# Opening, last unit and tail of a fused attention and recurrent layer: rotation halves interleaved, key stack split, two batches' output products moved

## Time and profile before

| | |
|---|---|
| median of three runs | 5033.72 us (5031.82 to 5034.27) |
| profiled execution | 5053.02 us, span 5051.2 us |
| mean granted PE clock | 0.986 |
| PE busy | 4895.6 us (97%) |
| DVE busy | 3960.6 us (78%) |
| ACT busy | 2884.9 us (57%) |
| POOL busy | 2930.4 us (58%) |

### The profile page before, as it was taken

How to read it: one execution, slowest core, us unless ns; L and a number is a source line. 1 busy time by engine, 2 the same in 40 slices (tenths; PEclk the granted TensorE clock), 3 DMA queues, 4 the chain that set the end, 5 groups by cost and what they waited for, 6 DMA issues and landing times.

```text
span 5051.2 us, 67243 instructions
## 1 busy us (share of the span) xinstructions
PE 4895.6 (97%) x24784; PEld 1745.4 (35%) x24784; DVE 3960.6 (78%) x6295; ACT 2884.9 (57%) x5221; POOL 2930.4 (58%) x2134
## 2 busy tenths in 40 slices
PE   7999999999999999999999999999999999999999
PEld 2224242332424233242332424233242433324237
DVE  7888878888887878878887887888788787887526
ACT  1565646656465665646566464665646566564642
POOL 3583837657374674728567383764738477472740
PEclk7899999999999999999999999999999999999999
DMA  6121222303122130222313123230312313022117
GB/s 151 30 56 52 47 66 53 66 32 66 47 47 72 34 76 38 55 59 47 72 34 62 46 47 70 48 66 30 67 48 47 72 34 76 39 47 55 68 51 291
DMA packets 127867, 311.19 MB, mean 62 GB/s; under 512 B 27313, under 2 KB 30514, under 8 KB 113714
## 3 DMA queue, kind: packets, MB, share of 16 engines
q1 hardware_dynamic: 124562, 289.72, 24.1%
q10 hardware_dynamic: 2976, 17.17, 0.9%
HBM read 172.07 MB, written 99.61 MB: 54 GB/s over the span
## 4 chain that ended last, share of the span: by engine, by line
PE 77%; POOL 11%; ACT 5%; DVE 3%; issue 3%; DMA 0%; SPq 0%; ACTq 0%; DVEq 0%; POOLq 0%
PE s_ps L795 15%; PE o_ps L835 15%; PE st L822 14%; PE st L928 13%; POOL pair_sum L484 11%; PE sum_ps L850 7%; PE st L763 4%; PE st L781 4%; ACT probs L591 3%; DVE neg_max L1127 2%; PE st L1005 2%; PE st L906 1%; PE o_ps L750 1%; DVE xa L1114 1%; PE s_ps L1005 1%
## 5 line engine op out<-in xcount | busy, mean ns | idle before, releaser
L484 POOL TENSOR_TENSOR pair_sum<-probs 128x512 f32<-128x512 f32 x2048 | 2822.1, 1414 | 1211.3 <-ACT probs L591 1210.6
L1127 DVE TENSOR_REDUCE neg_max<-s_ps 128x1 f32<-128x512 f32 x4096 | 2582.1, 682 | 700.2 <-PE s_ps L795 697.8
L591 ACT ACTIVATE probs<-st 128x512 f32<-128x512 f32 x4096 | 2162.3, 603 | 971.6 <-PE st L822 810.6
L795 PE MATMUL s_ps<-k_stack,q_stack 96*128 96x512 bf16 x4096 | 1523.0, 389 | 43.5 <-DVE neg_max L1127 37.0
L822 PE MATMUL st<-q_stack,k_stack 99*128 99x512 bf16 x4096 | 1475.8, 385 | 28.7 <-ACT probs L591 7.5
L835 PE MATMUL o_ps<-probs,values 128*32 128x512 f32 x8192 | 1095.3, 607 | 12.2 <-ACT probs L591 8.5
L822 PEld LDWEIGHTS st<-q_stack,k_stack 99*128 99x128 bf16 x4096 | 368.3, 97 | 1360.1 <-ACT probs L591 905.2
L795 PEld LDWEIGHTS s_ps<-k_stack,q_stack 96*128 96x128 bf16 x4096 | 400.7, 98 | 686.0 <-DVE neg_max L1127 336.6
L850 PE MATMUL sum_ps<-pair_sum,ones 128*32 128x512 f32 x4096 | 534.9, 594 | 26.6 <-POOL pair_sum L484 26.6
L928 PE MATMUL st<-pair_sum,weights 128*128 128x512 f32 x768 | 381.9, 594 | 11.8 <-ACT pair_sum L547 11.8
L541 ACT ACTIVATE probs<-st,gate_bias 128x512 f32<-128x512 f32 x192 | 131.7, 686 | 441.7 <-PE st L928 441.7
(11 more groups left out here) (151 smaller groups left out, 2926.6 us busy)
## 6 DMA issues: line engine op xcount, KB each, us to landing
q_stack<-qk_parts SPq DMA_DIRECT2D x384, 128.0 KB, 4.3
k_stack<-qk_parts SPq DMA_DIRECT2D x381, 128.0 KB, 7.0
swapped<-xa SPq DMA_DIRECT2D x128, 256.0 KB, 2.4
qk_parts<-swapped SPq DMA_DIRECT2D x64, 512.0 KB, 2.8
qk_parts<-low_part SPq DMA_DIRECT2D x64, 256.0 KB, 3.0
probs<-in_x SPq DMA_DIRECT2D x16, 1024.0 KB, 9.7
x_rows<-probs SPq DMA_DIRECT2D x16, 1024.0 KB, 3.9
xa<-in_x SPq DMA_DIRECT2D x15, 1024.0 KB, 6.0
```

What stands on the lines that cost most here:

```text
L484: pool.tensor_tensor(pair_sum[q % 2][:, h, :], probs[a % 4][:, h, :], probs[(a + 1) % 4][:, h, :], ALU.add)\
L591: act.activation(probs[kk % 4][:, h, :], st[n % BANKS][:, :], ACT.Exp).then_inc(exp_done, 1)
L795: pe.matmul(s_ps[i % BANKS][:, :], q_stack[g][0:SROWS, s, t * P:(t + 1) * P], k_stack[g][0:SROWS, s, h * HALF:(h + 1) * HALF], start=True, ...
L1127: dve.tensor_reduce(neg_max2[:, at, i % 2:i % 2 + 1], s_ps[i % BANKS][:, :], AX.X, ALU.max, negate=True).then_inc(max_done, 1)
```

## The change

- Opening: unit 0's two halves are rotated interleaved on DVE, step order 0, 1, 2, 7, 8, 4, 9, 6, 11, 13. ACT makes all four casts before the two `take_first`. k's low part goes to a buffer of its own (`first_low`, in `probs[0]`), so it waits for no store. The first half of unit 0's key stack is loaded by sub-head: six loads of sub-head 0 (32 KB), then six of sub-heads 2, 4, 6 (96 KB), three and three each on SP and ACT. The first 16 scores wait for the first six and q's stack, the rest as before.
- Last unit: the z products of batches 0 and 1 (eight groups) are made on PE into `s_ps`, three between the turned maximum and the last key sum of unit 30, five behind the steps 3, 9, 15, 21, 27 of unit 31. DVE copies each to SBUF (`keep_z`): batch 0 to `xt`, batch 1 to the row slot 3, whose row load is therefore made in the tail. The columns of batches 4 and 5 are loaded when the batches 0 and 1 are done.
- Tail: it begins with batch 2. DVE makes batches 0 and 1 with one add each over 2048 columns from the kept products, ahead of batch 2's.

```diff
+Z_AT = {3: 3, 9: 4, 15: 5, 21: 6, 27: 7}
+Z_FIRST, Z_BESIDE = 3, 2
...
+        first_low = probs[0][:, 0, :].bitcast(BF16)
...
+        z_beside = [flat(xt), tail_x[3]]
...
+        def first_stack(engine, blocks):
+            for subs, landed in ((slice(0, 1), first_keys), (slice(2, SUBS, 2), stack_in[1][0])):
+                for i in blocks:
+                    engine.dma_start(k_stack[0][D * i:D * i + D, subs, :],
+                                     qk_scr[1, K_PART[i], :, :].rearrange("(j d) t -> d j t", d=D)
+                                     [:, subs, :]).then_inc(landed, 16)
...
-                    for s in range(4):
+                    for s in range(3):
                         tail_load(s, s)
+                    for k in range(Z_BESIDE):
+                        sp.wait_ge(tail_z, 4 * (k + 1))
+                        tail_columns(k + COLS)
...
             store_part(0, 1)
-            stack(0, 0, 0, (1,), range(BLK // 2))
+            sp.wait_ge(parts_out[1], 32)
+            first_stack(sp, range(BLK // 2))
             swap(1, 1, 0)
...
             sp.wait_ge(x2_out, 16 * (NB + 1))
+            sp.wait_ge(tail_add, 4 * Z_BESIDE)
+            tail_load(3, 3)
             for k in range(NB):
-                if k + COLS < NB - 1:
+                if k >= Z_BESIDE and k + COLS < NB - 1:
...
-            for step in (3, 5):
+            for step in (3, 5, 10, 12):
                 part_of(0, step)
-            take_first(0)
-            for step in (10, 12):
-                part_of(0, step)
-            take_first(1)
+            for X in range(2):
+                take_first(X)
             act.wait_ge(parts_out[1], 32)
-            for i in range(BLK // 2, BLK):
...
+            first_stack(act, range(BLK // 2, BLK))
...
+                if u == 0 and i == 2 * TT:
+                    stacked(u, 0)
...
+            def z_group(n):
+
+                k, j = divmod(n, 4)
+                bank = s_ps[(n + 1) % BANKS]
+                if n == 0:
+                    pe.wait_ge(z_in, 32)
+                if n == 2:
+                    pe.wait_ge(shift_made, 2 * NB)
+                if n >= BANKS:
+                    pe.wait_ge(z_kept, n - BANKS + 1)
+                if j == 0:
+                    pe.wait_ge(tail_cols[k], 16)
+                for t in range(2):
+                    for c in range(KC):
+                        at = c * T + (2 * j + t) * P
+                        mm = pe.matmul(bank[:, t * E:(t + 1) * E], tail_t[k][:, at:at + P],
+                                       weights[:, W_Z, c, :], start=(c == 0), stop=(c == KC - 1))
+                mm.then_inc(tail_z, 1)
...
                     key_tile(u, g, s, 3)
                     for i in todo[3:]:
                         score(un, 1 - g, i)
+                    if z_at is not None and s in z_at:
+                        z_group(z_at[s])
...
                 turn_max(u + 1)
                 if not last:
                     qk(1, b, ab)
+                else:
+                    for n in range(Z_FIRST):
+                        z_group(n)
                 key_sums(u, 0, 15)
...
-            pe.wait_ge(z_in, 32)
-            z_rows(0)
+            z_rows(Z_BESIDE)
             pe.wait_ge(cell_ready, 4 * NB + 1)
...
-            for k in range(1, NB):
+            for k in range(Z_BESIDE + 1, NB):
                 z_rows(k)
...
-                        dve.tensor_tensor(low_part[:, :], raw[X], high_parts[X][:, 1, :],
+                        dve.tensor_tensor(first_low if n == 1 else low_part[:, :], raw[X], high_parts[X][:, 1, :],
...
+            def keep_z(n):
+
+                k, j = divmod(n, 4)
+                dve.wait_ge(tail_z, n + 1)
+                dve.tensor_copy(z_beside[k][:, 2 * j * E:2 * (j + 1) * E],
+                                s_ps[(n + 1) % BANKS][:, :]).then_inc(z_kept, 1)
...
                 split_shift(u + 1)
+                if last:
+                    for n in range(Z_FIRST):
+                        keep_z(n)
                 finish_sums(u, 0, 3)
...
-            rope(0)
+            rope(0, (0, 1, 2, 7, 8, 4, 9, 6, 11, 13))
...
+                if k < Z_BESIDE:
+                    dve.wait_ge(z_kept, 4 * (k + 1))
+                    dve.tensor_tensor(tail_n[k % 6], z_beside[k], x2, ALU.add)\
+                       .then_inc(tail_add, 4)
+                    if k >= 1:
+                        tail_finish(k - 1, slice(0, TT * E), k)
+                    continue
                 for j in range(4):
```

More of the change, by code:

```diff
@@ L195, in build @@
         first_rows = sem("first_rows")
+        first_keys = sem("first_keys")
         xr_in = sem("xr_in")
@@ L243, in build @@
         tail_z = sem("tail_z")
+        z_kept = sem("z_kept")
         tail_add = sem("tail_add")
@@ L296, in store_part @@
                   .then_inc(parts_out[X], 16)
-                sp.dma_start(qk_scr[X, 2, :, :], low_part[:, :]).then_inc(parts_out[X], 16)
+                sp.dma_start(qk_scr[X, 2, :, :], first_low if 2 * u + X == 1 else low_part[:, :])\
+                  .then_inc(parts_out[X], 16)
             def store_parts(u):
@@ L679, in take_first @@
                     take(0, QK1 + 2 * X + h, raw[X][:, h * HALF:(h + 1) * HALF])
-            for step in (3, 5):
+            for step in (3, 5, 10, 12):
                 part_of(0, step)
-            take_first(0)
-            for step in (10, 12):
-                part_of(0, step)
-            take_first(1)
+            for X in range(2):
+                take_first(X)
             act.wait_ge(parts_out[1], 32)
-            for i in range(BLK // 2, BLK):
-                act.dma_start(k_stack[0][D * i:D * i + D, 0:SUBS:2, :],
-                              qk_scr[1, K_PART[i], :, :].rearrange("(j d) t -> d j t", d=D)
-                              [:, 0:SUBS:2, :]).then_inc(stack_in[1][0], 16)
+            first_stack(act, range(BLK // 2, BLK))
             take_v(0, range(VAL[0], PRE), range(4))
@@ L804, in score_start @@
             def score_start(u):
-                stacked(u, 0)
+                if u > 0:
+                    stacked(u, 0)
+                else:
+                    pe.wait_ge(stack_in[0][0], 16 * BLK)
+                    pe.wait_ge(first_keys, 16 * BLK)
                 if not (isinstance(u, int) and u == 0):
@@ L852, in key_sums, with attention @@
                 mm.then_inc(sum_done, 1)
-            def attention(u, g, un, plan):
+            def z_group(n):
[15 more added lines that the diff above has]
+                mm.then_inc(tail_z, 1)
+            def attention(u, g, un, plan, z_at=None):
                 pe.wait_ge(shift_in, 48 * (u + 1))
@@ L892, in iteration @@
                     pe.wait_ge(act_out, ab + QK1 + 4)
-                attention(u + 1, 1, u + 2, NO_PLAN if last else PLAN1)
+                attention(u + 1, 1, u + 2, NO_PLAN if last else PLAN1, Z_AT if last else None)
                 late = iter(range(SCORES - sum(LATE), SCORES))
@@ L993, in z_rows @@
             def z_rows(k):
+                if k == Z_BESIDE:
+                    pe.wait_ge(z_kept, 4 * Z_BESIDE)
                 columns = flat(xt2) if k == NB - 1 else tail_t[k % COLS]
@@ L997, in z_rows @@
                 for j in range(4):
-                    if k == 0 and j < 3:
+                    if k == Z_BESIDE and j < 3:
                         turn(GEE + j, NB - 1, act_base(NB - 1, True))
-                    if k > 0:
+                    if k > Z_BESIDE:
                         pe.wait_ge(tail_add, 4 * (k - 1) + (j + 1))
@@ L1117, in rope @@
                         dve.wait_ge(part_made[X], 2 * u + 2)
-                        if n > 0:
+                        if n > 1:
                             dve.wait_ge(parts_out[1 - X], 32 * ((n + 1) // 2))
-                        dve.tensor_tensor(low_part[:, :], raw[X], high_parts[X][:, 1, :],
+                        dve.tensor_tensor(first_low if n == 1 else low_part[:, :], raw[X], high_parts[X][:, 1, :],
                                           ALU.subtract).then_inc(rope_done, 1)
@@ L1192, in finish_sums, with attention @@
                 combine(u, g, r)
-            def attention(u, g, un, plan, turned=None):
+            def keep_z(n):
[3 more added lines that the diff above has]
+                                s_ps[(n + 1) % BANKS][:, :]).then_inc(z_kept, 1)
+            def attention(u, g, un, plan, turned=None, z_at=None):
                 for s in range(STEPS):
@@ L1212, in attention @@
                         rope(turned, [ROPE_AT[g][s]])
+                    if z_at is not None and s in z_at:
+                        keep_z(z_at[s])
             def iteration(b, last):
@@ L1221, in iteration @@
                 split_shift(u + 1)
+                if last:
+                    for n in range(Z_FIRST):
+                        keep_z(n)
                 finish_sums(u, 0, 3)
                 attention(u + 1, 1, u + 2, NO_PLAN if last else PLAN1,
-                          None if last else u + 3)
```

(1 more changed line is left out.)

## The result

The changed kernel took 5043.18 us (median of 17 runs, 5040.69 to 5049.28) against 5033.72 for the kernel before in the same rounds (17 runs, 5031.46 to 5039.82): **ratio 1.0019, 95% interval 1.0012 to 1.0025**, so 9.5 us slower. The forecast was 5044.7, range 5028 to 5051. The loss is at the 0.2% that I called just measurable; the interval lies wholly above 1, so it is a loss.

A forecast was written before the change was run, and what follows sets the result against it. PE, holding 77% of the chain, was taken as the bound, with savings counting only where PE or what it waits for is next. Opening -0.9, joint +11.1, unit 31 +6.5, tail -5.7 gave +11.0: 5033.7 to 5044.7 us, range 5028 to 5051.

The forecast's parts named there:

- Opening: Start up to the second batch's statistics: they start at 93.75 instead of 94.63, -0.9 us (bounds -4.1 and +0.5).
- joint: Passage into unit 31: three z groups wait for columns and run slow ahead of it, +11.1 us (bounds +8 and +13).
- unit 31: Last unit: five groups on PE each delay the next tile by 1.29 us, +6.5 us (bounds 0 and 8.7).
- tail: Output products: two batches fewer -13.8, DVE's head work +6.7, slow clock +1.4, together -5.7 us (bounds -8 and -4).
- K's store landing: Opening: K's store stays behind the Q loads and lands at 47.6 instead of 46.43; 45.6 if its issue decided.
- The fourth V group: Opening, on PE: 1.99 us behind ACT's value copy, scores 2.1 us earlier; only 0.6 if PE lost its clock.
- POOL and x[1]: Opening: POOL's rotation 1.8 us later, x[1] landing at 93.75 instead of 91.95, with DVE waiting for it as a sign.
- The 8 us wait: Joint: PE idles 8 us from 4759.5 until the first column load, issued behind the shift rows, lands at 4767.6.
- The rival in which POOL's pace hides them: Unit 31 hides its groups and late start: +1.1 instead of +17.6, sum -5.5, 5028.2 us; chance 0.12.
- A gap of 8.2 us ended by batch 2's sum: Tail: PE stands 8.2 instead of 1.5 us behind the gate product while DVE makes batches 0 and 1 first.
- Transfers in the tail: Tail rival: 35.7 MB of transfers bind, last stores land 2 us later, +13, 5046.7 us; chance 0.06.
- The rival in which all but the removed products is hidden: Columns arrive before PE needs them, DVE's head work runs beside the gate product: -14.7, 5019.0 us; chance 0.10.

The follow-up runs named there:

- e5: e1 with K's store issued ahead of the loads of Q's stack on SP; 5032.30 us, ratio 0.9996 to the kernel before.
- e3: The changed kernel with the last iteration's four column loads issued ahead of the shift rows on SP; 5032.07 us, ratio 0.9999 to the kernel before.
- e6: e4 with SP reloading the row slots in the order in which the batches are stored; 5038.31 us, ratio 1.0007 to the kernel before.
- e7: The changed kernel with the edits of e3, e5 and e6 together; 5024.77 us, ratio 0.9978 to the kernel before.
- e4: The changed kernel with batch 2's sum ahead of the two kept batches on DVE, stores reordered alike; 5042.15 us, ratio 1.0018 to the kernel before.
- e1: The changed kernel's opening alone, with the last unit and tail of the kernel before; 5034.23 us, ratio 1.0002 to the kernel before.
- e8: e7 with unit 31's five groups moved: three ahead of weighted products, two among the closing sums; 5026.85 us, ratio 0.9981 to the kernel before.
- e9: e7 with the opening's query half loaded like its key half, sub-head 0 first; ratio 0.9977 to the kernel before.
- e12: e9 with the stalling DVE add moved from attention step 16 to 15, its input's cast to 13; ratio 0.9972 to the kernel before.
- e11: e9 with the stalling DVE add moved from attention step 16 to 17, work behind it one step later; ratio 0.9951 to the kernel before.

## Why the prediction was right

- **What bounds it, and the three places**: held. Opening -0.1, joint +10.1 (11.7 later, 1.6 back), unit 31 +6.5, tail -6.7, against -0.9, +11.1, +6.5, -5.7 forecast. No term is off by more than 1.0, so the sum doesn't rest on large errors that cancel. The 19.3 us by which the profiled execution lay above the median were taken as all durations scaled by 0.4%; they are four long DVE adds instead (19.5 us, last section). The sum doesn't depend on it.
- **The opening.** K's store landing was forecast at 47.6 and measured at 47.78; e5 shows by its opposite that the Q loads ahead of it are the reason. Two terms were off. The fourth V group ran with the clock down (3.78 us; my text had that as a bound, 0.6 left, and it should have been the value). And POOL and x[1] came no later: the rotation started at 55.73, as before, since the swap, though issued 2.7 us later, had landed at 57.56 against 57.74: before, too, it had lain behind stack loads. So x[1] was issued at 83.95 and landed at 91.99 in both, and DVE didn't wait for it, though the prediction named that wait as a sign. By how much the opening gained is less sure than -0.1 sounds: unit 1's turned maximum is at 145.2 to 147.2 in the six traces with the changed opening (mean 146.3), at 146.5 and 147.1 in the two with the old one.
- **The joint.** The 8 us wait came as forecast (8.23). The products took 7.22 us and I had forecast 8.4: the granted clock was full from 4758, some 4 us behind the restart, and not the 6.3 that I took from the row with 0.50 6.9 us behind the earlier trace rows. That row is of a stretch where PE had waits between its products; here it had none. Whether that is the reason, no run tests.
- **Unit 31.** 1.29 for each group: right to 0.01 in each of the five. The rival in which POOL's pace hides them fell: POOL still waited for an exponential (16.0 us of idle time from 4770 to 4855, against 11.8).
- **The tail.** A gap of 8.2 us ended by batch 2's sum: measured 8.17. The product behind it took 7.46 us instead of 5.34, so about 2.1 us lost to the clock where I took 3.1; that is most of the 1.0 us by which the tail is better than forecast.
- **Transfers in the tail** bind nothing: from 4956.93 to the last batch's start at 5032.90 PE takes 11 x 6.91 us, without a wait, while the DMA engines move 426 GB/s from 4977 to 5017.
- **The rival in which all but the removed products is hidden** needed SP's and DVE's order to be no obstacle. They were, and e3 and e6 show that each is an obstacle of order alone. With both out of the way, and K's store first, e7 gains 9 us. Its trace against the kernel before: opening -4.0, joint +1.4, unit 31 +4.9, tail -12.1, together -9.8. It stays short of that rival's 14.7 because the groups in unit 31 still cost 6.5.

## What to carry to other kernels

Work moved from a full stretch of an engine into an idle one starts when its inputs are there, not when the engine is free. Before moving it, move the loads that it needs ahead in the queue that issues them; here the order of two entries in SP's list was worth 10 to 11 us, where 13.8 us of work was moved. And when the head of a pipeline is rearranged, give the sum that releases the bounding engine the first place, with the stores and loads behind it reordered alike: e4 did the one without the other and gained nothing.

## What was not expected of the hardware

**One DVE add takes 1.28 or 6.20 us.** Two rows of the kernel before, in two units at the same place, 79.8 us behind the turned maximum, and PE behind the first of them (timeline rows):

```profile
3502.20 6.20 DVE L1114 TENSOR_TENSOR xa<-xa,swapped 128x1024 f32<-128x1024 f32 x1
...
3509.06 0.61 PE L795 MATMUL s_ps<-k_stack,q_stack 96*128 96x512 bf16 x1 [2.81 <-DVE neg_max L1127]
...
3806.29 1.28 DVE L1114 TENSOR_TENSOR xa<-xa,swapped 128x1024 f32<-128x1024 f32 x1
```

and POOL at both:

```profile
3498.65 8.68 POOL L484 TENSOR_TENSOR pair_sum<-probs 128x512 f32<-128x512 f32 x7
...
3802.74 9.66 POOL L484 TENSOR_TENSOR pair_sum<-probs 128x512 f32<-128x512 f32 x7
```

The add reads two tiles in SBUF. These are the last seven sums of a run of 28 that POOL makes without a gap. They take 8.68 us where the add takes 6.20, and 9.66 where it takes 1.28: either POOL yields about a microsecond or DVE gets through only when POOL's run is over (3507.3; the add ends at 3508.4). So it is in every trace: where the add is long, POOL's run is 42.4 us and the add ends 1.1 us behind it (28 times); where it is short, the run is 43.3 to 43.4 us and the add ends 4.8 us ahead of its end. The scores wait for the maxima behind the add, PE stands 2.8 us, and its clock falls to 0.50 from 3510 to 3514. One such event costs 3.5 to 6.3 us of a unit. In the fourteen traces (both kernels and twelve experiments) 28 of DVE's 1024-column instructions beside attention took longer than 2.6 us; all are this add, at 6.18 to 6.20 us, 0 to 8 in an execution: 27 of the 196 at this place, and one in e5's unit 1. The four traces of e1 to e4 have none, those of e5 to e8 four, those of e9 to e12, on the chips where the kernel before took 5053 and 5056 us, nineteen. That accounts for the difference of the two profiled spans, and fits the scatter of the runs. The Trainium skill (GPSIMD Engine Reference, 1. Specifications) says that GpSimd's SBUF interfaces are shared with VectorE, with contention for DVE instructions that have two SBUF inputs; the trace agrees that there is contention, and shows in addition that at this place it has these two outcomes and nothing between. At other places beside attention DVE's instructions of the same shape on the same tiles take 1.3 to 2.3 us. What decides between the two stays open, and so does why the long one was rarer on some chips than on others. The time at which the add comes is not it: in both outcomes it starts 37.27 to 37.29 us behind the start of POOL's run. And e11 and e12 did not move it in time.

**Pieces of 2 KB.** A stack load moves rows of 1024 bf16 values, 2 KB each. In e5 and e9 as in the kernel before, such loads keep the DMA engines full at only some 130 to 190 GB/s, where whole blocks reach 426. What is issued behind them waits: unit 1's swap, issued at 45.76 in e5 behind eighteen stack loads, has its first part in at 53.89, 8.1 us later; in e9 it is issued at 42.94, with nine small loads in front, and its first part is in at 45.43, 2.5 us later.
